# Three buffers of q and k in the attention, the stack of a head loaded one head earlier, its maxima over all 15 rounds

## The reference, cut to what matters

```python
att = jnp.einsum('bhqd,bhkd->bhqk', q, k) * scale
att = jnp.where(causal, att, -jnp.inf)
att = jax.nn.softmax(att, axis=-1)
y = jnp.einsum('bhqk,bhkd->bhqd', att, v)
```

## Time and profile before

| what | value |
|---|---|
| time, median of 3 runs | 4264.32 us (4262.82 to 4269.22) |
| profiled execution, first to last instruction | 4268.8 us |
| mean granted TensorE clock | 0.949 |
| busy: PE / DVE / POOL / ACT | 90% / 65% / 65% / 42% |
| DMA | 549.12 MB, mean 129 GB/s |

### The profile page before, as it was taken

How to read it: one execution, slowest core, us unless ns; L and a number is a source line. 1 busy time by engine, 2 the same in 40 slices (tenths; PEclk the granted TensorE clock), 3 DMA queues, 4 the chain that set the end, 5 groups by cost and what they waited for, 6 DMA issues and landing times. The chain is left out here.

```text
span 4268.8 us, 81098 instructions
## 1 busy us (share of the span) xinstructions
PE 3857.2 (90%) x21344; PEld 2337.8 (55%) x21344; DVE 2754.6 (65%) x5889; ACT 1806.6 (42%) x3526; POOL 2780.5 (65%) x2251
## 2 busy tenths in 40 slices
PE   5989999987999999879899999879899999859998
PEld 2754544456744454457554544457545444547776
DVE  3767677466757767476667776567676774645655
ACT  1345555423355555332355555233455555211111
POOL 3768788824668878716678888427687888215554
PEclk8989999998999999989899999889899999979999
DMA  6543333242533333334433333425333332349997
GB/s 210 180 119 91 91 99 108 79 181 98 178 93 100 86 102 96 120 135 148 139 91 100 99 98 108 155 82 179 115 90 91 99 105 81 102 135 258 258 257 190
DMA packets 305135, 549.12 MB, mean 129 GB/s; under 512 B 59572, under 2 KB 99636, under 8 KB 301492
## 3 DMA queue, kind: packets, MB, share of 16 engines
q1 hardware_dynamic: 283192, 485.62, 37.8%
q0 software_dynamic: 21504, 58.40, 5.8%
HBM read 311.86 MB, written 174.85 MB: 114 GB/s over the span
## 5 line engine op out<-in xcount | busy, mean ns | idle before, releaser
L1141 ACT ACTIVATE Pt<-PS 128x512 f32<-128x512 f32 (+3 forms) x2560 | 1205.9, 542 | 1004.6 <-PE PS L1334 554.9
L1006 POOL TENSOR_TENSOR Sm<-Pt 128x512 f32<-128x512 f32 (+3 forms) x960 | 1029.5, 1078 | 389.6 <-ACT Pt L1141 383.6
L1653 DVE TENSOR_REDUCE part<-PS 128x1 f32<-128x512 f32 x1536 | 1003.5, 685 | 334.6 <-PE PS L1311 329.6
L1311 PE MATMUL PS<-QK 96*128 96x512 f32 (+3 forms) x2560 | 1026.8, 419 | 88.6 <-DVE mT L1668 24.4
L1334 PE MATMUL PS<-QK 97*128 97x512 f32 (+3 forms) x2560 | 991.8, 409 | 38.7 <-DMA QK<-mT 18.5
L1358 PE MATMUL PS<-Pt,V 128*32 128x512 f32 (+3 forms) x5120 | 870.0, 554 | 42.5 <-POOL Sm L1006 42.3
L1362 PE MATMUL PS<-Sm,onesv 128*32 128x512 f32 (+3 forms) x1920 | 818.8, 535 | 0.0
L1649 DVE CUSTOM_DVE_ANT_0 PS<-PS,consts 128x128 f32<-128x128 f32 (+3 forms) x1024 | 503.8, 495 | 415.8 <-PE PS L1311 408.5
L1334 PEld LDWEIGHTS PS<-QK 97*128 97x128 f32 x2560 | 488.0, 193 | 474.7 <-issue 345.7
L1006 POOL TENSOR_TENSOR Sm<-Sm,Pt 128x512 f32<-128x512 f32 (+1 forms) x640 | 713.2, 1114 | 50.2
L1311 PEld LDWEIGHTS PS<-QK 96*128 96x128 f32 x2560 | 496.0, 195 | 299.5 <-DVE part L1653 110.8
(11 more groups left out here) (169 smaller groups left out, 4962.6 us busy)
## 6 DMA issues: line engine op xcount, KB each, us to landing
QK<-qkd SPq DMA_DIRECT2D x720, 128.0 KB, 3.1
qkd<-st SPq DMA_DIRECT2D x64, 1024.0 KB, 4.5
Wg<-wgu SPq DMA_DIRECT2D x48, 768.0 KB
o<-od SPq DMA_DIRECT2D x448, 64.0 KB, 2.0
W<-wd SPq DMA_DIRECT2D x3, 6144.0 KB, 21.5
Wd<-wdn SPq DMA_DIRECT2D x48, 384.0 KB
xin<-x SPq DMA_DIRECT2D x16, 1024.0 KB, 7.9
vd<-vst SPq DMA_DIRECT2D x16, 1024.0 KB, 6.1
```

Source lines behind the costliest of these rows:

```text
L1006: nc.gpsimd.tensor_tensor(total, of[0][:, first:CH] if i == 1 else total, of[i][:, first:CH], ALU.add).then_inc(sum_done, 1)
L1141: nc.scalar.activation(Pt[:, t % NPT, first:CH], S2[t % NS2][:, first:CH], ACT.Exp, scale=SCALE).then_inc(exp_done, 1)
L1311: mm(s1[:, 0:w], QK[0:3 * HD, hh % 2, 0, qb * P:(qb + 1) * P], QK[0:3 * HD, hh % 2, 1, c * CH:c * CH + w], start=True, stop=True).then_inc ...
L1653: v.reduce_max(part[:, qb, cc:cc + 1], s1[:, 0:w], AX.X).then_inc(s1_dve, 1)
```

## The change

It adds a third buffer `QK2` (placed where `xin0` and `vst1` of the front stage lie) and uses buffer `hh % 3`. SP loads the stack of head `hh+1` where it loaded that of head `hh` before, under the same wait; at `hh` = 1 it loads both head 1 and head 2. The maxima of head `hh` are spread from round 0 to round 14 of head `hh-1` (for head 1 from round 4 to 14). POOL's `second` also waits for the stores of `vst1` and sets two rows of ones. `x1` and `xn`, `h2` of the routing stage change places.

```diff
+NBUF = 3
-TILES_FROM = 2
 FIRST_TILES_FROM = 4
     for hh in range(1, H):
-        late = TILES_FROM if hh > 1 else FIRST_TILES_FROM
-        at, span = NR * (hh - 1) + late, NR + 1 - late
+        late = 0 if hh > 1 else FIRST_TILES_FROM
+        at, span = NR * (hh - 1) + late, NR - late
         for i in range(NTILE):
             beside[at + i * span // NTILE].append(("max", hh, i))
             if i in (FIRST_HALF - 1, NTILE - 1):
...
+        at[0] = XIN_AT
+        QK2 = place("QK2", [P, 2, T], F32R)
+        QKB = [QK[:, 0], QK[:, 1], QK2]
...
-        x1 = place("x1", [P, 2, TPC, C], F32)
         xn = place("xn", [P, TPC, C], F32)
         h2 = place("h2", [P, TPC, C], F32)
+        x1 = place("x1", [P, 2, TPC, C], F32)
...
                     if hh >= 2:
 
                         wait_apart(sp, s2_ready, NPT_B * b + NTILE * (hh - 1))
-                    if hh < H:
-                        for j in range(NCH):
-                            stack(hh, j, qkd[b, g, h * HD:(h + 1) * HD, :, j * CH:(j + 1) * CH])
+                    if hh == 1:
+                        load_stack(1)
+                    if hh + 1 < H:
+                        load_stack(hh + 1)
                     max_row(hh - 1, 1)
...
                         wait_apart(pool, rope_mul, 2 * NCK * (b + 1))
-                        nc.gpsimd.memset(QK[3 * HD:3 * HD + 1, 1, 1, :].bitcast(F32), 1.0).then_inc(ones_set, 1)
-                        wait_apart(pool, ones_set, 3 * b + 3)
+                        wait_apart(pool, v_out[1], 32 * (NCH // 2) * (b + 1))
+                        for i in range(1, NBUF):
+                            nc.gpsimd.memset(QKB[i][3 * HD:3 * HD + 1, 1, :].bitcast(F32), 1.0).then_inc(ones_set, 1)
+                        wait_apart(pool, ones_set, 4 * b + 4)
```

More of the change, by code:

```diff
@@ L97, with stacked @@
 NCK = NCH * NG
+def stacked(i):
+    return len(range(i, H, NBUF))
 def extent(j, k):
@@ L379, in adaln_block @@
         rsA = place("rsA", [P, TPC], F32)
+        XIN_AT = at[0]
         xin = [place("xin0", [P, TPC, C], F32), xin1]
@@ L539, in adaln_block @@
         v_in = [sem("v_in0"), sem("v_in1")]
-        qk_in = [[sem("qk_in%d%d" % (i, j)) for j in range(NCH)] for i in range(2)]
+        qk_in = [[sem("qk_in%d%d" % (i, j)) for j in range(NCH)] for i in range(NBUF)]
         s1_ready = sem("s1_ready")
@@ L697, in stack @@
                     for blk, pair in enumerate((parts[:, 0::2], parts[:, 1:3], parts[:, 0::3])):
-                        sp.dma_start(QK[blk * HD:(blk + 1) * HD, hh % 2, :, cols].bitcast(F32), pair).then_inc(qk_in[hh % 2][j], 16)
+                        sp.dma_start(QKB[hh % NBUF][blk * HD:(blk + 1) * HD, :, cols].bitcast(F32), pair).then_inc(qk_in[hh % NBUF][j], 16)
                 def store_parts(n):
@@ L735, in max_row @@
                     wait_apart(sp, mt_ready, 2 * (H * b + hh) + half + 1)
-                    sp.dma_start(QK[3 * HD:3 * HD + 1, hh % 2, 0, half * (T // 2):(half + 1) * (T // 2)].bitcast(F32),
+                    sp.dma_start(QKB[hh % NBUF][3 * HD:3 * HD + 1, 0, half * (T // 2):(half + 1) * (T // 2)].bitcast(F32),
                                  mT[:, half].bitcast(F32)).then_inc(mrow_in[half], 16)
@@ L787, in _, with load_stack @@
                     wait_apart(sp, v_out[i], 32 * (NCH // 2) * (b + 1))
+                def load_stack(hh):
+                    g, h = divmod(hh, GH)
+                    for j in range(NCH):
+                        stack(hh, j, qkd[b, g, h * HD:(h + 1) * HD, :, j * CH:(j + 1) * CH])
                 for hh in range(1, H + 1):
@@ L916, in _ @@
                 meet(pool, 2 * b + 1)
-                nc.gpsimd.memset(QK[3 * HD:3 * HD + 1, 0, 1, :].bitcast(F32), 1.0).then_inc(ones_set, 1)
-                wait_apart(pool, ones_set, 3 * b + 1)
+                nc.gpsimd.memset(QKB[0][3 * HD:3 * HD + 1, 1, :].bitcast(F32), 1.0).then_inc(ones_set, 1)
+                wait_apart(pool, ones_set, 4 * b + 1)
                 nc.gpsimd.memset(part[:, :, :], -3e38).then_inc(ones_set, 1)
@@ L1116, in _ @@
                         if g == 2:
-                            act.wait_ge(qk_in[0][j], ONE + 48 * (H // 2 * b + 1))
+                            act.wait_ge(qk_in[0][j], ONE + 48 * (stacked(0) * b + 1))
                         nc.scalar.activation(st[n % 2][:, 0::2], t1[:, n % 2], ACT.Copy).then_inc(q_hi, 1)
@@ L1308, in _ @@
                         if qb % TPC == 0 and c == 0:
-                            pe.wait_ge(qk_in[hh % 2][qb // TPC], ONE + 48 * (H // 2 * b + hh // 2 + 1))
-                        mm(s1[:, 0:w], QK[0:3 * HD, hh % 2, 0, qb * P:(qb + 1) * P], QK[0:3 * HD, hh % 2, 1, c * CH:c * CH + w],
+                            pe.wait_ge(qk_in[hh % NBUF][qb // TPC], ONE + 48 * (stacked(hh % NBUF) * b + hh // NBUF + 1))
+                        mm(s1[:, 0:w], QKB[hh % NBUF][0:3 * HD, 0, qb * P:(qb + 1) * P], QKB[hh % NBUF][0:3 * HD, 1, c * CH:c * CH + w],
                            start=True, stop=True).then_inc(s1_ready, 1)
@@ L1323, in _ @@
                             if hh == 1:
-                                wait_apart(pe, ones_set, 3 * b + 3)
+                                wait_apart(pe, ones_set, 4 * b + 4)
                             if hh == 0:
-                                wait_apart(pe, ones_set, 3 * b + 2)
+                                wait_apart(pe, ones_set, 4 * b + 2)
                                 pe.wait_ge(f_act, ONE + N_QT * (b + 1))
@@ L1333, in _ @@
                             pe.wait_ge(exp_done, ONE + NPT_B * b + t - NS2 + 1)
-                        last = mm(S2[t % NS2][:, first:CH], QK[0:3 * HD + 1, hh % 2, 1, k * P:(k + 1) * P],
-                                  QK[0:3 * HD + 1, hh % 2, 0, j * CH + first:(j + 1) * CH], start=True, stop=masked == 0)
+                        last = mm(S2[t % NS2][:, first:CH], QKB[hh % NBUF][0:3 * HD + 1, 1, k * P:(k + 1) * P],
+                                  QKB[hh % NBUF][0:3 * HD + 1, 0, j * CH + first:(j + 1) * CH], start=True, stop=masked == 0)
                         if masked:
@@ L1642, in _ @@
                         if hh == 0 and i == 0:
-                            wait_apart(dve, ones_set, 3 * b + 2)
+                            wait_apart(dve, ones_set, 4 * b + 2)
                         s1 = S1[n1 % NS1]
```

## The result

The changed kernel takes 4389.59 us (median of 4 runs, 4367.82 to 4404.35) against 4263.57 us for the kernel before: a ratio of 1.029, 95% interval 1.0257 to 1.0324. That is 126 us slower where 38 were forecast; the sign was right, the size three times too small, and the time lies outside the range of 4272 to 4340. The profiled execution spans 4377.9 us, 109 more than before, and its mean granted clock is 0.933 instead of 0.949.

The account below looks back on a forecast made before the run. PE was taken as the limit between small waits, with the copied row setting the entry. Entry 31, stack -15, maxima and row steps 11, POOL 7 and head 0 4 gave +38 us: 4302 us, range 4272 to 4340.

Parts of the forecast that it names:

- The entry: Start of attention in each batch: 12 more loads ahead of the copied row of maxima, +31 us over four batches.
- transfer alone counts: Entry, before head 0's round 5: PE's wait near 8 us, not some 12.5, would mean only the loads' transfer time matters.
- The stack: Pair 1 of odd heads: the third buffer brings the next head's stack earlier and removes PE's wait, -15 us.
- POOL takes gains back: Heads 3, 7, 11: PE's gains in pairs 7 to 13 return as longer waits for POOL's sums, +7 us.
- the term of the maxima and the row steps: Heads 1 to 14: moved row steps and maxima cost +0.4 us per two heads, +11 us in all.
- late `row`: Row step late in a pair, priced at 1.10 us from head 2's pair 6, against 0.36 for an early one.
- rival 3: More short PE waits lower its granted clock in 20 of 56 heads: 34 us, 4336 us in all; 16%.
- Head 0: Three more maxima in pairs already holding 7, where DVE is slower: 1 us a batch, 4 us in all.
- every `row` at the early price: Heads 1 to 14: lower bound of the row and maxima cost, -0.5 us for two heads, -14 us in all.
- rival 2: Entry: the second twelve loads are cheaper than the first, costing 16 us, 4287 us in all; 8%.

Follow-up runs that it names:

- the old spread: Changed kernel with three buffers and earlier loads, but maxima and row steps placed as in the kernel before: 4277.54 us, ratio 1.0034 to the kernel before.
- the earlier copy: Changed kernel with head 2's stack loaded behind the copy of head 0's second row of maxima: 4358.3 us, ratio 1.0226 to the kernel before.
- the fill: Changed kernel with the second product behind pair 0's late row step computed four times in even heads: 4336.81 us, ratio 1.0174 to the kernel before.

## Why the forecast of slower was right and its size wrong

**What held.** The entry: forecast 31, measured 30 in the trace and 28 to 31 by the experiment; that the medians give 31 exactly is luck, since their runs overlap. SP's queue took 15.46 us from the first load to the copy, as forecast. The sign that a wait of PE near 8 us would mean "transfer alone counts" was wrong, though: the wait was 8.48 because POOL's longer `second` held PE up by 4.7 us beside the late copy. In time it cost nothing there, as the prediction had it, because the copy came last. The stack: -15 forecast, -20 measured. Single pairs at full clock: pair 6 5.63 (forecast 5.4), odd pair 5 5.62 (5.3 to 5.7), odd pair 13 4.54 (4.4), pair 2 4.03 (4.1 to 4.4), pair 0 5.52 (5.1; 28 x 0.4 = 11 us of the error). POOL takes gains back as forecast, and more: pair 13 of heads 3, 7 and 11 grew by 7.5 us in all, where the two terms together had it fall by 1, and it does so in another pair too. Pair 10 fell from 4.96 to 4.32 us in head 2 and rose from 4.95 to 5.12 in head 4, behind a group:

```profile
361.82:366.14 4.32, 4.32 (x33) 2.57 (x30) 2.64 (x7) 3.64 (x7) 3.46 (x4) 1.00 0.01 4
439.43:444.55 5.12, 4.53 (x34) 2.41 (x30) 2.64 (x7) 3.64 (x7) 4.96 (x6) 1.00 0.15 54
```

**What failed: the term of the maxima and the row steps, and POOL's beside it, both with the clock at nothing.** The prediction priced a late `row` once, "late `row`, pair 6 of head 2, 6.06 us, against pair 10 [...]: 1.10", and carried this to pair 0 of the even heads. The terms gave +11 us for heads 1 to 14, +7 for POOL and +4 in head 0. Measured against the old spread, they are 112 us. In the traces heads 1 to 14 grew by 69 us although the stack's wait gave 20 back, so there the terms are 89 and not 18: 47 of them half clock in pairs 0 and 2, and 42 the rest, which is within the prediction's bounds of 35 and 14. So the price 1.10 holds at full clock, but PE's idle time also lowers the clock, for that pair and the next. The sum had nothing for that.

**Where the argument broke.** The clock was rival 3, with 16% and 34 us. Against it the prediction put "the waits of 0.84 and 1.28 us in heads whose clock stayed at 1.00". Those waits stand one at a time, and one of the 28 pairs 6 of the even heads did fall in the kernel before, 0.4 us after its wait of 0.85 us (head 14 of batch 0). In pair 0 of the even heads there are two within 2 us, in a pair of narrow products; with just these two waits 12 of 22 pairs 0 fell, and with the longer one filled none of 25. In pair 13 of heads 3, 7 and 11 the 1.28 us became two waits of 2.1 to 2.5 us in 6 of 12 places, and there the clock fell each time (in 8 of 9 with the earlier copy, in 3 of 4 with the fill). That longer wait is what the prediction's own term for POOL forecast ("what PE gains in pairs 7 to 13 comes back as a longer wait"); it priced the wait and not the clock. Odd pair 5 has the late `row` among wider products, idles 0.70 us in head 1, and kept its clock in all 28 cases of heads 1 to 13. What sets the pairs that fall apart from those that don't stays open: head 14 has the same two waits in pair 0 and fell in no batch. That the width of the products matters is read from these counts; it was not tried apart. That POOL's double wait starts the other falls is read from their place in the traces; no run takes this wait away alone.

The Trainium skill ("TensorE: Matmul & The Clock Gate", section "A second HAM failure mode: psum-queue depth-cycling") says that frequent short idling between groups of matmuls makes the clock swing between its levels. The prediction held this against most heads showing 1.00; the rows of head 12 at 0.50 and the fill experiment now agree with it for pairs 0 and 2.

**Head 0** cost 9 us behind its pair 4 (forecast 4, bound 7), nearly all in its pairs 8 (5.79 to 6.99 us in the middle) and 10 (5.43 to 6.11), which hold 7 and 8 maxima where they held 6 and 7; the tails took 6 and were costed at nothing. With the `row` moved from pair 8 to pair 10, pair 8 is back at 5.78 us and pair 10 rises to 6.83, so how this splits between row and crowd stays open.

**Sums that don't come out.** The lower bound of -0.5 for two heads ("every `row` at the early price") would be -1.1 by the prediction's own prices (1.44 - 2.08 - 0.70 + 0.25), and the upper one of +1.25 would be +1.1; neither changes the forecast. PE's busy time does not fill every pair without a `row`: pair 13 of head 1 in the earlier trace rows has 5.03 of 5.24 us.

## What to carry to other kernels

A wait's price belongs to the place where it will stand: before carrying it over, look at the other waits next to it, at the width of the products around it, and at the granted clock of just those stretches, since a mean over the kernel moved by 0.016 only. A prefetch put into a queue delays every urgent transfer behind it by its whole issue time, so the small copy that somebody waits for goes first. When a change bundles a resource and a new order, try the resource with the old order: here the buffer with the old order, and with the small copy ahead of the second stack, was a gain of 0.4%, and the new order a loss of 112 us.

## What the runs showed of the hardware that was not expected

Adding 84 products made the kernel 53 us faster, because they kept PE's clock up. A stretch once at half clock carries it into the next pair: pair 2 of head 12 has no wait of PE at all (busy 6.87 of 6.87 us) and ran at 0.53, and in the fill experiment no pair 2 was at half clock, though nothing was changed in it. And 24 loads of 128 KB in one queue took 15.2 to 15.9 us in batch 0, twice the 7.5 to 8.0 us of 12 loads: the second run of loads is not cheaper than the first, which settles rival 2.
